# Merging the two experts' rows on TensorE before they are added to memory, two planes instead of four, and fourteen unread products

## The chip, the cores and the metric

The kernel runs on one core of one Trainium2 chip. The metric is the device time of one execution in microseconds; the time before is the median of three runs. The profile is one execution recorded by the hardware profiler; TensorE's clock has two levels in it, 1.2 GHz (granted clock 0.5) and 2.4 GHz (1.0).

## The reference, cut to what matters

The block is macaron shaped: x + 0.5 FFN(LN(x)), then x + attention(LN(x)), then x + 0.5 FFN(LN(x)), for 8 sequences of 512 tokens with 128 channels (T = 4096 tokens). The FFN is a mixture of 64 experts of inner width 88, 6 per token, plus a shared expert of width 176:

```python
scores = softmax(xf @ gate_w.T)
_, idx = top_k(scores + gate_b, 6)
# per expert, its tokens in token order; only the first CAP = 64 are kept
h  = silu(einsum('ecd,eid->eci', xb, w1)) * einsum('ecd,eid->eci', xb, w3)
yb = einsum('eci,edi->ecd', h, w2)
y  = zeros_like(xf).at[tok].add(contrib * wf[:, None])   # scatter-add by token
z  = silu(xf @ ws1.T) * (xf @ ws3.T) @ ws2.T
return (y + z).reshape(shape)
```

So each expert gives 64 rows of 128 numbers, each row is weighted with its token's score and added to its token. Two experts can hold the same token.

## The kernel before, in words

Each engine runs its own program in order; semaphores join them. `ffn(f)` stands in the program of TensorE (PE), VectorE (DVE) and ScalarE (ACT), and a loop over `f` in those of GpSimd (POOL) and SyncE (SP); f is 0 and 1 for the first and second FFN.

Routing: `norm` normalises in four groups of 1024 columns, `xT` and `logits` give the scores, DVE's `top` the six largest, and then, in four quarters h of 16 experts, `scan(h)` (DVE), `differences(h)` (PE, L722), `table(h)` (DVE, L1050), `look_up(h)` (PE, L732) and `slots(h)` (DVE, L1057) find each expert's 64 tokens. `slots` writes `tok_i`, from which POOL gathers rows, and `put_i`, where POOL adds rows. Quarters 0 and 1 run ahead of the expert turns, 2 and 3 inside turns 0 to 3.

The expert stage has 32 slots of two experts, 2s and 2s+1, on partitions 0 to 63 and 64 to 127, in NS + 2 = 34 turns (the loops at L782, L1110 and L574). In turn s PE turns the gathered rows (`xb_turn(s)`, L758), makes the hidden products of slot s-1 (`hidden`, L769) and the output products of slot s-2 (`expert_out`, L778); ACT copies the turned rows (L566) and does the silu (L572); DVE does `gate(s-1)` (L1083) and `weigh(s-2)` (L1106, two instructions of 64x128), whose semaphore `y_sb` lets POOL add the slot's 128 rows. PE waits for `y_sb` only two turns later, when it writes the bank again. The shared expert lies between: from turn 8 on, of every four turns the first two end with `shared_hidden(g, 0)` and `(g, 1)` (L705), each followed by ACT's silu (L560) and DVE's `shared_gate` (L1094), and the third with `shared_out(g)` (L718), followed by DVE's `shared_add` (L1099); the fourth has nothing. `shared_hidden(g, 1)` waits for the gate of `(g, 0)`, and `shared_out(g)` for that of `(g, 1)`. Groups 6 and 7 are made during routing (L705), multiplied in turns 3 and 4 (L1090) and brought out in turns 32 and 33.

POOL's queue is one in-order list (L458 to L470): ten gathers ahead (L466), then add(0) (L452), gather 10, add(1), and so on; the last ten adds follow each other. Each is an indirect DMA of 128 rows. Adds that may be in flight together must not meet on one row, so each token has four rows in `planes_d`: plane 2 (s mod 2) + (expert mod 2). SP zeroes the planes (`clear_planes`, 2 MB per plane): planes 0 and 1 of f = 0 at the start, 2 and 3 ahead of most of the expert weights, all four of f = 1 behind the reads of f = 0. After the last add has landed SP reads the planes in four groups of 2 MB (L345), and DVE's `update` adds each group's four planes to X (L957, four instructions of 128x1024), with statistics and normalisation behind them in the first FFN, and the store of the output (L366) behind them in the second.

## Time and profile before

| | us |
|---|---|
| median of 3 runs (lowest, highest) | 533.45 (532.67, 536.54) |
| the profiled execution | 532.9 |
| its span | 531.2 |
| PE, DVE, ACT, POOL busy in the span | 356.6, 307.6, 207.8, 237.0 |
| mean granted TensorE clock | 0.793 |

The profiled execution took 532.9 us, 1.7 us more than its span, and 0.55 us less than the median. Stages, by the time line: first FFN to 212, attention to 341, second FFN to the end; expert turns from 59 to 154 and from 396 to 489.

### The profile page before, as it was taken

The numbers are of one execution on the slowest core, as the hardware profiler recorded it, in microseconds if no ns is written. First come the engines' busy times: TensorE is split into PE (matmuls) and PEld (weight loads), VectorE is DVE, ScalarE is ACT, GpSimd is POOL, SyncE is SP. The second block draws the span as 40 slices with busy tenths as digits, with TensorE's granted clock in tenths as the row PEclk, the third lists the DMA queues.
The fourth block names the chain that finished last, engine by engine and source line by source line (L and its number), as shares of the span: only waits on it lengthen the run. The fifth ranks groups of instructions, "written<-read, shape, count | busy, mean of one in ns | idle before, by whom it ended". The sixth has DMA issues, their size and how long they took to land.

```text
span 531.2 us, 14693 instructions
## 1 busy us (share of the span) xinstructions
PE 356.6 (67%) x5808; PEld 263.3 (50%) x5812; DVE 307.6 (58%) x999; ACT 207.8 (39%) x543; POOL 237.0 (45%) x215
## 2 busy tenths in 40 slices
PE   0874589999960013598999999218848999998000
PEld 0851475666650012376788888118327667666000
DVE  6488363545430994454777775394985544545077
ACT  3983112322310067744677762169722232231000
POOL 7161747887872000403333333001537888887400
PEclk9987567999995556678999999657855699999555
DMA  8999961001015996000111111454200100100396
GB/s 272 369 268 341 318 185 15 5 11 14 5 6 218 407 401 239 2 2 2 40 40 40 40 40 49 109 218 139 61 8 8 12 11 6 17 5 6 108 426 257
DMA packets 49746, 62.64 MB, mean 118 GB/s; under 512 B 21701, under 2 KB 36248, under 8 KB 47183
## 3 DMA queue, kind: packets, MB, share of 16 engines
q1 hardware_dynamic: 37423, 60.51, 33.3%
q0 software_dynamic: 12288, 1.70, 3.2%
q8 instruction: 17, 0.28, 0.2%
q14 instruction: 18, 0.15, 0.1%
HBM read 39.53 MB, written 31.46 MB: 134 GB/s over the span
## 4 chain that ended last, share of the span: by engine, by line
PE 53%; DVE 23%; DMA 9%; ACT 6%; issue 5%; POOL 3%; SPq 1%; POOLq 0%; DVEq 0%; ACTq 0%
PE bank L769 6%; PE upper L864 5%; PE bank L705 5%; DVE X L957 5%; PE bank L718 5%; PE upper L705 4%; DMA Cb<-planes_d 4%; PE upper L778 3%; DVE Cb L1094 3%; DVE bn L962 3%; DVE Cb L1025 3%; POOL planes_d L452 3%; ACT Cb L560 2%; ACT A L508 2%; PE bank L880 2%
## 5 line engine op out<-in xcount | busy, mean ns | idle before, releaser
L452 POOL DMA_INDIRECT planes_d<-Bb,put_i x64 | 101.4, 1584 | 28.0 <-issue 14.8
L480 POOL TENSOR_TENSOR Bb<-Cb,chm 128x576 f32<-128x576 f32 x32 | 36.9, 1183 | 124.3 <-PE upper L909 69.6
L466 POOL DMA_INDIRECT A<-rows_d,tok_i x64 | 68.0, 1063 | 41.6 <-DVE put_i L1066 22.7
L672 PE MATMUL bank<-ident,A 128*128 128x128 f32 x96 | 21.3, 396 | 81.9 <-ACT A L508 65.1
L672 PEld LDWEIGHTS bank<-ident,A 128*128 128x128 f32 x96 | 17.0, 209 | 85.1 <-ACT A L508 52.3
L1106 DVE TENSOR_SCALAR Bb<-upper,A 64x128 f32<-64x128 f32 x128 | 44.4, 347 | 1.3
L1094 DVE TENSOR_TENSOR Cb<-Cb,upper 88x512 f32<-88x512 f32 x24 | 16.4, 683 | 44.8 <-ACT Cb L560 44.8
L769 PEld LDWEIGHTS bank<-ring,w1s 128*88 128x88 f32 x256 | 34.2, 191 | 8.0 <-issue 8.0
L433 POOL TENSOR_TENSOR Bb<-Eb,st 128x512 f32<-128x512 f32 x8 | 8.3, 1043 | 63.8 <-DVE st L1013 63.8
L560 ACT ACTIVATE Cb<-bank 88x512 f32<-88x512 f32 x24 | 14.2, 592 | 55.1 <-PE upper L705 55.1
L769 PE MATMUL bank<-ring,w3s 128*88 128x64 f32 x256 | 35.6, 270 | 0.0
L705 PE MATMUL bank<-XT,ws1s 128*88 128x512 f32 x56 | 32.1, 656 | 3.7 <-DVE Cb L1094 3.7
L769 PE MATMUL bank<-ring,w1s 128*88 128x64 f32 x256 | 34.1, 264 | 0.0
L1083 DVE TENSOR_TENSOR ring<-ring,bank 88x128 f32<-88x128 f32 x64 | 18.0, 281 | 26.2 <-ACT ring L572 26.1
L778 PE MATMUL upper<-w2s,ring 88*64 88x128 f32 x256 | 31.4, 328 | 0.1
L864 PE MATMUL upper<-A,Bb 32*32 32x128 f32 x1024 | 30.8, 273 | 1.0 <-issue 1.0
L769 PEld LDWEIGHTS bank<-ring,w3s 128*88 128x88 f32 x256 | 30.2, 185 | 0.0
L615 ACT ACTIVATE A<-Bb,hm 128x512 f32<-128x512 f32 x32 | 20.5, 711 | 24.1 <-PE upper L864 22.2
L705 PE MATMUL upper<-XT,ws3s 128*88 128x512 f32 x56 | 29.8, 615 | 0.0
L508 ACT ACTIVATE A<-X,st 128x128 f32<-128x128 f32 x72 | 28.6, 481 | 0.0
L957 DVE TENSOR_TENSOR X<-X,A 128x1024 f32<-128x1024 f32 x8 | 9.8, 1225 | 31.5 <-DMA A<-planes_d 31.3
L718 PE MATMUL bank<-ws2s,Cb 88*128 88x128 f32 x192 | 24.6, 281 | 3.9 <-DVE Cb L1094 3.6
(162 smaller groups left out, 804.7 us busy)
## 6 DMA issues: line engine op xcount, KB each, us to landing
planes_d<-zeros SPq DMA_DIRECT2D x8, 2048.0 KB, 15.9
rows_d<-A SPq DMA_DIRECT2D x8, 512.0 KB, 6.0
A<-planes_d SPq DMA_DIRECT2D x4, 1024.0 KB, 6.0
PL<-planes_d SPq DMA_DIRECT2D x4, 1024.0 KB, 10.0
Bb<-planes_d SPq DMA_DIRECT2D x4, 1024.0 KB, 13.7
Cb<-planes_d SPq DMA_DIRECT2D x4, 1024.0 KB, 18.0
w1s<-in_w1T SPq DMA_DIRECT2D x4, 704.0 KB
w3s<-in_w3T SPq DMA_DIRECT2D x4, 704.0 KB
```

The lines of the kernel that those rows point to most:

```text
L452: pool.indirect_dma_start(out=planes_d[f], in_=Y[:, s, :], in_offset=None, out_offset=bass.IndirectOffsetOnAxis(ap=put_i[:, s:s + 1], axis=0),
L466: pool.indirect_dma_start(out=GAT[:, t % RING, :], out_offset=None, in_=rows_d, in_offset=bass.IndirectOffsetOnAxis(ap=tok_i[:, t:t + 1], ...
L480: pool.tensor_tensor(out=VX[:, :, :, c, :].rearrange("p q h f -> p (q h) f"), in0=VN.rearrange("p q h f -> p (q h) f"), in1=chm[:, c:c + 1 ...
L508: ins = act.activation(A[:, i, :], X[:, i, :], ACT.Identity, bias=st[:, 1, i:i + 1], scale=st[:, 4, i:i + 1])
L672: ins = pe.transpose(bank[g % 2][:, (i % 4) * P:(i % 4 + 1) * P], A[:, i, :], ident[:, :])
L705: ins = pe.matmul(bank[bk][0:I, :], w[:, k * I:(k + 1) * I], XT[:, 512 * g:512 * g + 512], start=True, stop=True)
L718: ins = pe.matmul(bank[SHARED[0]][:, i * D:(i + 1) * D], hs(g)[k][:, i * P:(i + 1) * P], ws2s[:, k, :], start=(k == 0), stop=(k == 1))
L769: ins = pe.matmul(bank[2 + s % 2][0:I, cols], w[:, 2 * s + k, :], XBT[s % 2][:, CAP * k:CAP * k + CAP], start=True, stop=True)
L778: ins = pe.matmul(bank[(4, 7)[s % 2]][CAP * k:CAP * k + CAP, 0:D], GT[s % 2][:, CAP * k:CAP * k + CAP], w2s[:, 2 * s + k, :], start=True, ...
L864: ins = pe.matmul(bank[4 + g][CHUNK * c:CHUNK * c + CHUNK, q * P:(q + 1) * P] .rearrange("p (j t) -> p j t", j=4), KT[rows, t0:t0 + CHUNK] ...
L957: then(dve.tensor_tensor(xt, xt, PLANES[g].rearrange("p (i k d) -> p i k d", i=GI, k=4)[:, :, k, :], ALU.add))
L1106: ins = dve.tensor_scalar(Y[rows, s, :], bank[(4, 7)[s % 2]][rows, 0:D], GAT[rows, s % RING, col:col + 1], 0.5, ALU.mult, ALU.mult)
```

## The change

What it does:

- PE's turn becomes `xb_turn(s)`, `expert_out(s-2)`, `hidden(s-1)`, `merge(s-2)`. `merge` is one new product of 64x64 by 64x128: a matrix SAME of zeros and ones, which says which row of the second expert has the token of which row of the first, times the second expert's weighted rows. It waits for the new semaphore `weighed`, which DVE's `weigh` raises.
- DVE's turn becomes `weigh(s-2)`, `gate(s-1)`, `add_second(s-2)` (new, 64x128: the product plus the first expert's rows, which raises `y_sb`), and the rest. `weigh` no longer multiplies by 0.5.
- SAME is made per quarter: `spread(h)` (DVE, 64x512) ahead of `table(2)` and in turns 4, 10, 18; `token_rows(h)` (PE, 64x64 by 64x512) in turns 0, 5, 11, 19; `match(h)` (DVE, a compare of 64x512 from PSUM, a maximum over it, two small instructions) in turns 1, 6, 11, 19. A row of the second expert that was merged gets an index beyond the planes, and its write is dropped.
- Two planes instead of four: SP zeroes and reads half as much, the 4 MB of zeros ahead of the expert weights are gone, and `update` has two `scalar_tensor_tensor` (times 0.5, plus X) instead of four adds. The number of indirect DMAs stays.
- `keep_busy(n)` issues n products of `ident` (128x128) by 512 columns of XT into bank 2, which nobody reads: 4 ahead of `differences(0)`, 2 behind each of `differences(0)`, `look_up(0)`, `differences(1)` and `look_up(1)`, and 2 in turn 0.
- `look_up(3)` moves from turn 2 to turn 3, `table(3)` from turn 2 to turn 1 behind `slots(2)`.

```diff
+    SPREAD, ROW_TURN, MATCH = (4, 10, 18), (5, 11, 19), (6, 11, 19)
...
-        planes_d = [nc.dram_tensor(f"planes{f}_d", (4 * T, D), F32, kind="Internal").ap() for f in range(2)]
+        planes_d = [nc.dram_tensor(f"planes{f}_d", (2 * T, D), F32, kind="Internal").ap() for f in range(2)]
...
-            clear_planes(sp, 0, (0, 1))
+            clear_planes(sp, 0)
...
                 if f == 0:
-                    clear_planes(sp, 0, (2, 3))
                     for h in range(1, NQT):
...
+                            pe.wait_ge(same_ready, NQT * f + (2, 3, 3, 4, 4, 4)[g])
...
+                def keep_busy(n):
+                    for _ in range(n):
+                        pe.matmul(bank[2][:, :], ident[:, :], XT[:, 0:512], start=True, stop=True)
+
+                keep_busy(4)
                 for h in range(2):
                     differences(h)
+                    keep_busy(2)
                     look_up(h)
+                    keep_busy(2)
...
+                def token_rows(h):
+                    pe.wait_ge(rows_set, NQT * f + h + 1)
+                    if NQT * f + h:
+                        pe.wait_ge(same_ready, NQT * f + h)
+                    ss = slice(QSL * h, QSL * h + QSL)
+                    pe.matmul(bank[LOOK[1]][CAP:P, :], ones[:, :], ROWS[:, ss, :].rearrange("p s c -> p (s c)"),
+                              start=True, stop=True).then_inc(rows_ps, 1)
+
+                def merge(s):
+                    if s % QSL == 0:
+                        pe.wait_ge(same_ready, NQT * f + s // QSL + 1)
+                    pe.wait_ge(weighed, f * NS + s + 1)
+                    pe.matmul(bank[(4, 7)[s % 2]][0:CAP, D:2 * D], SAME[:, s, :], Y[CAP:P, s, :], start=True, stop=True)\
+                        .then_inc(merged, 1)
...
                 for s in range(NS + 2):
                     if s < NS:
                         xb_turn(s)
+                    if s == 2:
+                        pe.wait_ge(dr_sb, NQT * (f + 1))
+                    if s == 3:
+                        pe.wait_ge(table_ready, NQT * (f + 1))
+                    if s >= 2:
+                        expert_out(s - 2)
                     if 1 <= s <= NS:
                         hidden(s - 1)
-                    if s == 2:
-                        pe.wait_ge(dr_sb, NQT * (f + 1))
                     if s >= 2:
-                        expert_out(s - 2)
+                        merge(s - 2)
+                    if s in ROW_TURN:
+                        token_rows(1 + ROW_TURN.index(s))
                     if s == 0:
+                        keep_busy(2)
                         differences(2)
                         look_up(2)
+                        token_rows(0)
                     elif s == 1:
                         differences(3)
-                    elif s == 2:
+                    elif s == 3:
                         look_up(3)
...
-                    for k in range(4):
-                        then(dve.tensor_tensor(xt, xt, PLANES[g].rearrange("p (i k d) -> p i k d", i=GI, k=4)[:, :, k, :], ALU.add))
+                    for k in range(2):
+                        then(dve.scalar_tensor_tensor(xt, PLANES[g].rearrange("p (i k d) -> p i k d", i=GI, k=2)[:, :, k, :], 0.5,
+                                                      xt, ALU.mult, ALU.add))
...
+                def match(h):
+                    ss = slice(QSL * h, QSL * h + QSL)
+                    dve.wait_ge(rows_ps, NQT * f + h + 1)
+                    then(dve.tensor_tensor(SAME[:, ss, :], bank[LOOK[1]][CAP:P, :].rearrange("p (s c) -> p s c", s=QSL),
+                                           sl[CAP:P, 1, ss].unsqueeze(2).broadcast_to([CAP, QSL, CAP]), ALU.is_equal))
+                    then(dve.tensor_reduce(sl[CAP:P, 0, ss], SAME[:, ss, :], AX, ALU.max))
...
-                    ins.then_inc(y_sb, 1)
+                    ins.then_inc(weighed, 1)
+
+                def add_second(s):
+                    dve.wait_ge(merged, f * NS + s + 1)
+                    dve.tensor_tensor(Y[0:CAP, s, :], bank[(4, 7)[s % 2]][0:CAP, D:2 * D], Y[0:CAP, s, :], ALU.add).then_inc(y_sb, 1)
 
                 for s in range(NS + 2):
+                    if s >= 2:
+                        weigh(s - 2)
                     if 1 <= s <= NS:
                         gate(s - 1)
+                    if s == 1:
+                        match(0)
                     if s >= 2:
-                        weigh(s - 2)
+                        add_second(s - 2)
                     if s == 1:
                         slots(2)
-                    elif s == 2:
                         table(3)
                     elif s == 3:
                         slots(3)
+                    elif s in SPREAD:
+                        spread(1 + SPREAD.index(s))
+                    elif s in MATCH:
+                        match(1 + MATCH.index(s))
```

## Rows read from the trace of the kernel before

**Rows 1.** Time line (start, length, engine, operation, [idle <- its end]): adds, weighs, first gather

```profile
153.01 0.70 DVE L1106 TENSOR_SCALAR Bb<-upper,A 64x128 f32<-64x128 f32 x2
...
161.58 1.55 POOL L452 DMA_INDIRECT planes_d<-Bb,put_i  x1 [0.30 <-issue]
...
393.32 1.08 POOL L466 DMA_INDIRECT A<-rows_d,tok_i  x1 [11.36 <-DVE put_i L1066]
...
488.73 0.70 DVE L1106 TENSOR_SCALAR Bb<-upper,A 64x128 f32<-64x128 f32 x2
...
497.00 1.55 POOL L452 DMA_INDIRECT planes_d<-Bb,put_i  x1 [0.31 <-issue]
```

**Rows 2.** Busy time by stretch: PE, PEld, DVE, ACT, POOL, then PEclk, DMA share, GB/s

```profile
393.30:419.30 26.00, 21.99 (x155) 17.34 (x156) 16.11 (x47) 5.76 (x19) 21.10 (x17) 0.50 0.09 12
419.30:489.40 70.10, 65.73 (x481) 45.01 (x480) 34.87 (x96) 18.16 (x59) 56.55 (x44) 0.99 0.08 9
```

**Rows 3.** Time line behind the first FFN's adds

```profile
164.36 0.80 SPq L345 DMA_DIRECT2D A<-planes_d  x2
...
171.75 5.00 DVE L957 TENSOR_TENSOR X<-X,A 128x1024 f32<-128x1024 f32 x4 [15.76 <-DMA A<-planes_d]
...
201.81 3.19 ACT L508 ACTIVATE A<-X,st 128x128 f32<-128x128 f32 x8
...
207.17 1.92 ACT L503 ACTIVATE XT<-bank 128x512 f32<-128x512 f32 x2 [0.40 <-PE bank L672]
```

**Rows 4.** Time line behind the second FFN's adds

```profile
499.75 0.81 SPq L345 DMA_DIRECT2D A<-planes_d  x2
...
507.29 5.00 DVE L957 TENSOR_TENSOR X<-X,A 128x1024 f32<-128x1024 f32 x4 [15.58 <-DMA A<-planes_d]
...
523.01 5.00 DVE L957 TENSOR_TENSOR X<-X,Cb 128x1024 f32<-128x1024 f32 x4 [0.36 <-DMA Cb<-planes_d]
528.08 0.06 DVE L958 MEMSET st<- 128x1 f32 x1
```

**Rows 5.** Time line of four turns at full clock, first FFN

```profile
102.11 2.05 PE L718 MATMUL bank<-ws2s,Cb 88*128 88x128 f32 x16 [0.32 <-DVE Cb L1094]
...
104.00 0.27 PE L758 MATMUL upper<-ident,A 128*128 128x128 f32 x1
...
104.20 0.69 DVE L1099 SCALAR_TENSOR_TENSOR X<-bank,X 128x512 f32<-128x512 f32 x1 [1.32 <-PE bank L718]
...
105.22 0.28 DVE L1083 TENSOR_TENSOR ring<-ring,bank 88x128 f32<-88x128 f32 x1 [0.33 <-ACT ring L572]
...
106.41 1.09 PE L705 MATMUL bank<-XT,ws1s 128*88 128x512 f32 x2
...
108.39 0.59 ACT L560 ACTIVATE Cb<-bank 88x512 f32<-88x512 f32 x1 [1.98 <-PE upper L705]
...
109.02 0.68 DVE L1094 TENSOR_TENSOR Cb<-Cb,upper 88x512 f32<-88x512 f32 x1 [1.66 <-ACT Cb L560]
...
109.76 1.09 PE L705 MATMUL bank<-XT,ws1s 128*88 128x512 f32 x2 [0.32 <-DVE Cb L1094]
109.82 0.71 DVE L1106 TENSOR_SCALAR Bb<-upper,A 64x128 f32<-64x128 f32 x2
```

**Rows 6.** Time line of routing in the second FFN

```profile
384.93 0.58 ACT L543 ACTIVATE PL<-bank 88x512 f32<-88x512 f32 x1
...
387.91 0.19 PE L725 MATMUL upper<-Eb,before_b 128*128 128x16 bf16 x1 [3.51 <-DVE Eb L1046]
...
394.31 1.15 PE L739 MATMUL upper<-A,Bb 128*64 128x33 bf16 x16 [2.43 <-DVE Bb L1054]
...
395.63 0.45 PE L758 MATMUL bank<-ident,A 128*128 128x128 f32 x1 [0.16 <-DMA A<-rows_d,tok_i]
```

**Rows 7.** Time line of one turn at half clock, its start and the next one's

```profile
71.63 0.48 PE L758 MATMUL bank<-ident,A 128*128 128x128 f32 x1
...
73.79 0.48 PE L758 MATMUL upper<-ident,A 128*128 128x128 f32 x1
```

More of the change, by code:

```diff
@@ L110, in macaron_kernel @@
         plane0 = sb("plane0", [P, NS])
+        ones = sb("ones", [CAP, CAP])
         gate_s = sb("gate_s", [P, NE])
@@ L289, in macaron_kernel, with clear_planes @@
         block = ctx.enter_context(nc.Block())
-        def clear_planes(queue, f, parts=range(4)):
-            for k in parts:
+        def clear_planes(queue, f):
+            for k in range(2):
                 dst = planes_d[f][k * T:(k + 1) * T, :].rearrange("(p a i) d -> p a (i d)", p=P, i=4)
@@ L422, in _ @@
                 count(c_of_p[k * CAP:(k + 1) * CAP, :], 0, [[0, 1]], 1)
-                count(plane0[k * CAP:(k + 1) * CAP, :], k, [[0, NS // 2], [2, 2]], 0)
+                count(plane0[k * CAP:(k + 1) * CAP, :], 0, [[0, NS // 2], [1, 2]], 0)
+            then(pool.memset(ones[:, :], 1.0))
             pool.iota(slot_ce[:, :, :], pattern=[[1, CAP], [0, NE]], base=0, channel_multiplier=0,
@@ L1065, in slots, with spread @@
                     dve.tensor_copy(tok_i[:, ss], sl[:, 1, ss])
-                    dve.scalar_tensor_tensor(put_i[:, ss], sl[:, 1, ss], 4.0, plane0[:, ss], ALU.mult, ALU.add)\
+                    dve.scalar_tensor_tensor(put_i[0:CAP, ss], sl[0:CAP, 1, ss], 2.0, plane0[0:CAP, ss], ALU.mult, ALU.add)\
                         .then_inc(tokens_ready, 1)
+                def spread(h):
+                    ss = slice(QSL * h, QSL * h + QSL)
+                    dve.tensor_tensor(ROWS[:, ss, :], ident[0:CAP, 0:CAP].unsqueeze(1).broadcast_to([CAP, QSL, CAP]),
+                                      sl[0:CAP, 1, ss].unsqueeze(2).broadcast_to([CAP, QSL, CAP]), ALU.mult).then_inc(rows_set, 1)
+                def match(h):
+                    ss = slice(QSL * h, QSL * h + QSL)
+                    dve.wait_ge(rows_ps, NQT * f + h + 1)
+                    then(dve.tensor_tensor(SAME[:, ss, :], bank[LOOK[1]][CAP:P, :].rearrange("p (s c) -> p s c", s=QSL),
+                                           sl[CAP:P, 1, ss].unsqueeze(2).broadcast_to([CAP, QSL, CAP]), ALU.is_equal))
+                    then(dve.tensor_reduce(sl[CAP:P, 0, ss], SAME[:, ss, :], AX, ALU.max))
+                    then(dve.scalar_tensor_tensor(sl[CAP:P, 0, ss], sl[CAP:P, 0, ss], float(T), sl[CAP:P, 1, ss], ALU.mult, ALU.add))
+                    dve.scalar_tensor_tensor(put_i[CAP:P, ss], sl[CAP:P, 0, ss], 2.0, plane0[CAP:P, ss], ALU.mult, ALU.add)\
+                        .then_inc(same_ready, 1)
                 scan(0)
```

28 lines of the change are left out of this document (20 added, 8 removed).

## The prediction

> **What bounds the kernel now.** I read the time line of POOL first, then the busy time by stretch, then PE's, ACT's and DVE's time line through four turns, and last what follows the final add. POOL decides both expert stages. In the second FFN it issues 32 gathers and 31 adds between its first gather at 393.32 and its last add at 497.00 [rows 1]; 103.7 us over 63 DMAs is 1.65 us each, and its busy 21.10 of 26.0 us and 56.55 of 70.1 us [rows 2] leave only the gaps of issue. The last `weigh` ends at 489.43 and the last add starts at 497.00, so PE and DVE are done 7.6 us early; in the first FFN 153.71 against 161.58, 7.9 us early [rows 1]. That lead is all that PE and DVE can lose for nothing. Behind the adds stand two stretches of DMA and DVE: 164.4 to 212 and 499.8 to 531.2 [rows 3, 4].
>
> **The part that gains: two planes.** Second FFN: 2 MB land 7.54 us after the issue (499.75 to 507.29), and the fourth group's sum starts at 523.01, so a group takes (523.01 - 507.29) / 3 = 5.24 us and 2.3 us are latency [rows 4]. With half the bytes the first sum starts at 499.75 + 2.3 + 2.6 = 504.7 and the last group lands near 499.75 + 2.3 + 4 x 2.6 = 512.6, a little later beside the stores; DVE has two instructions of 1.25 us per group instead of four (5.00 us [rows 4]), if `scalar_tensor_tensor` costs what `tensor_tensor` does (per element it does within 15%: 0.69 us for 512 columns [rows 5]). So DVE ends at about 515.5 instead of 528.1: **-12.6 us**. First FFN: 2.6 us earlier start likewise. DVE's four groups take (201.81 - 171.75) / 4 = 7.5 us each, of which 2.5 go; ACT then has 0.3 + 3.19 + 1.92 = 5.4 us per group [rows 3] against DVE's 5.05 and becomes the bound by a little. Laid out group by group, ACT's last copy comes 29.5 us behind the first sum, where it came 39.6 us (it ends near 211.4): -10.1, together **-12.7 us**. Bounds of both together: -20 (instruction 1.4 us, transfers not halved in time) to -27. The clears are behind the reads or gone; nobody waits for them. The 4 MB of zeros gone ahead of the weights may let the first gathers of the first FFN land sooner, 0 to 4 us; I take this against the delay that the unread products bring there, and put the sum at 0 (-2 to +2).
>
> **The part that costs, in the repeating four turns.** In the old order PE never waits for `weigh` of the same turn. In the new one `merge` waits for it, everything of the next turn is queued behind `merge` on PE, and `weigh` is queued on DVE behind the shared expert's gate of the turn before. Count from the first product of `shared_hidden` at 106.41 [rows 5]: ACT starts at +1.98, DVE's shared gate at +2.61 and ends at +3.29; `weigh` then takes 0.71: +4.0; `merge` can start at +4.05. PE has its own turn done at 1.8 + 1.2 = +3.0 (1.2 is half of 104.00 to 106.41, two turns), so it stands idle for 1.05. The merging product has no row of its own. Below: 0.11, a quarter of the 512-column product's half (1.09 us for two [rows 5]); above: 0.5, half of that product at half clock. I take 0.22, since 128 columns are a quarter of 512 and that product takes about 0.86. The next `shared_hidden` starts at +4.27 where it started at +3.35 (109.76): +0.92, and once more for `shared_out`. Behind `shared_out` (102.11) DVE's `shared_add` starts at +2.09 and ends at +2.78 [rows 5]; `weigh` +3.5, `merge` to +3.75; then a turn without a shared part, which is `expert_out`'s result 0.5, `weigh` 0.71, `merge` 0.22 and the turning product, about 1.6; so the next `shared_hidden` starts at +5.3 instead of +4.3. Four turns: 4.27 + 4.27 + 5.3 = 13.85 us instead of 11.0. POOL needs two DMAs a turn, 2 x 1.65 = 3.3 us, 13.2 in four turns, so even where gathers and adds alternate the turns become the slower side, and in the last ten adds POOL has little to do and only waits. Turns 11 and 19 have `token_rows` and `match` besides: a product of 0.86, a compare and a maximum of 64x512 near 0.68 each as the shared gate's [rows 5], and two small ones with waits, 1.85 us of DVE ahead of the next `weigh`; PE loses about 2.2 in each. From turn 8 to the last row: 6 x 2.85 + 2 x 2.2 = **+21.5 us** (bounds +16 with the cheap product, +26 with the dear one and `add_second` above the gate's 0.28).
>
> **The first eight turns.** Before, they take 395.63 to about 419.3, 23.7 us, at granted clock 0.50 [rows 2, 6], 2.16 us each [rows 7]. Added: two unread products (1.7 us at full clock), `token_rows(0)` (0.9 to 1.7), and `merge`s that wait for a DVE which has other things first: in turn 2 `match(0)`, `slots(2)` and `table(3)` (some 3.4 us of PE idle), in turns 4 and 5 `slots(3)` and the two pairs of shared gates (0.64 each; 2.4 and 2.0), in turn 7 `match(1)` (1.7). Laying all four engines out in order with these durations gives 34.9 us if the clock is 0.5 for most of it, and 29.7 us if it is full: +11 or +6. I take **+9**, nearer the half clock. In the trace PE is busy without a break from turn 3 to turn 8, and the clock stays at 0.50 until the shared products [rows 2, 7]; the new turns have fewer products per microsecond. The Trainium skill (TensorE: Matmul & The Clock Gate, Part 1) says that the throttle is the default and that sustained activity releases it; by that rule alone these turns would run at full clock before and after, which the 0.50 of the trace does not bear out. It is rival (d).
>
> **The unread products in routing.** One is a fp32 product of 512 columns, about 0.86 us at full clock and 1.7 at half. In the second FFN the first four can start when ACT ends at 385.51 and end at 388.95, where `differences(0)` ran at 387.91: +1.0. Two more, `look_up(0)`, two, `differences(1)`, two, `look_up(1)` follow one another at 0.6 and 1.15 us: `look_up(1)` starts at 396.4 instead of 394.31, and with two more `xb_turn(0)` starts at 399.2 instead of 395.63 [rows 6]: **+3.6** (bounds +1 if half of it hides, +10 if the clock drops among them). In the first FFN PE has to wait for the first gather anyway: 0, as above.
>
> **The sum.** Second FFN: 3.6 + 9 + 21.5 = 34.1 later for the last row; the add then starts 0.85 us behind it and not 7.6, so the last add moves by +27.4. First FFN: 0 + 9 + 21.5, less 7.9 - 0.85: +23.5. Planes: -12.7 - 12.6. Together +25.6. Against the profiled execution's 532.9 that is **558.5 us**; its distance to the median, 0.55, is left out.
>
> **Rivals.**
> (a) *POOL stays the bound* (the other side: faster). If the turns lose less than the lead, 6.7 to 7.0 us per stage, the last add does not move but for the later first gather, 1.5 to 2 us. Then 532.9 - 25.3 + 3.5 = 511. It needs the `merge` waits nearly free: 32 products of 0.22 alone use 7.0 up, so it would also take a full clock in the first turns, worth up to 8 us. For it: POOL is saturated now, and PE is at half clock for eight turns. Against it: the idle 1.05 behind each shared product follows from rows. 0.14.
> (b) *Half of it*: the gate opens in the first turns, `merge` is cheap, ACT and DVE pipeline better than I lay out. +15 per stage: 532.9 + 30 - 25 = 538. 0.08, half of it within 1%.
> (c) *The clock falls in the middle.* PE is busy for 65.7 of 70.1 us at 0.99 now [rows 2]; in the new cycle it has some 11.3 of 13.85. If two cycles of six run at half clock, each loses about 7 us (two shared turns and `shared_out` at twice 1.8): +28 over both stages, 586. 0.08.
> (d) *Full clock in the first turns.* The products ahead of and in turn 0 bring the clock to 1.0 and it stays there until turn 8: +6 instead of +9 per stage, 532.9 + 25.6 - 6 = 552.5. Against it stands the 0.50 through eight dense turns. 0.15.
> (e) My forecast, with its own range of 545 to 575: 0.55.
> The range 528 to 582 leaves out most of (a) and (c). Within 1% of 533, about what a measurement of this kernel can tell from no change: 0.05; faster 0.14; slower 0.81.
>
> **What would show it.** The chain of waits should have `merge` waiting for DVE's `weigh`, about 1 us in each of the two shared turns; PE's four turns 13.8 us; POOL idle behind `add_second`, some 25 us per stage, where it has none in the second FFN now; the last add less than 1 us behind the last row; then two sums per group at 1.25 us. The forecast is wrong if the cycle stays under 13.2 us, if POOL still has a queue of adds at turn 33, or if the rows behind the adds shrink by less than 20 us.

## The result and the profile after

| | before | after |
|---|---|---|
| median of 4 runs each (lowest, highest), us | 533.06 (532.35, 536.54) | 584.4 (578.84, 588.31) |
| ratio, with its 95% interval | | 1.0864 (1.0776 to 1.0951) |
| the profiled execution, its span | 532.9, 531.2 | 580.85, 579.1 |
| PE, DVE, ACT, POOL busy | 356.6, 307.6, 207.8, 237.0 | 429.6, 326.9, 209.0, 237.4 |
| mean granted clock | 0.793 | 0.850 |

Two of the four runs of after (587.96 and 588.31 us) ran in a slower state of the chip and are left out of the ratio and of what follows, as one run of experiment 7 and one of experiment 10 are left out of their ratios; the other two took 578.84 and 580.85 us. The forecast was 558.5 us in a range of 528 to 582: the direction was right, the size (+25.6) about half of what came (+47.9 by the two profiled executions), and 580.85 lies at the very end of the range.

POOL is no longer the bound. The groups of POOL and of the new product, line by line (columns: busy, mean ns, then idle just before and what ended it):

```profile
L464 POOL DMA_INDIRECT planes_d<-Bb,put_i x64 | 101.6, 1588 | 93.6 <-DVE Bb L1176 79.8 <-issue 11.1 <-DMA planes_d<-Bb,put_i 2.8
L478 POOL DMA_INDIRECT A<-rows_d,tok_i x64 | 68.1, 1063 | 44.9 <-DVE put_i L1113 26.6 <-issue 18.3
...
L808 PE MATMUL upper<-Bb,Eb 64*64 64x128 f32 x128 | 30.9, 326 | 37.1 <-DVE Bb L1170 36.8
```

The adds cost the same (1.59 us) but POOL now stands 79.8 us waiting for `add_second` (L1176). One line below is why: TensorE is idle for 37.1 us in front of `merge` (L808), 36.8 of them waiting for `weigh` (L1170). (A product of fp32 counts as two records, so x128 are 64 merges.)

The two parts of each expert stage, from `xb_turn(0)` to turn 8 and from there to the last row, answer to [rows 2]. Busy time by stretch: PE, PEld, DVE, ACT, POOL, then PEclk, DMA share, GB/s:

```profile
63.10:100.30 37.20, 31.96 (x161) 19.33 (x162) 19.25 (x55) 5.77 (x19) 20.04 (x17) 0.55 0.16 33
100.30:197.90 97.60, 83.49 (x531) 50.15 (x532) 47.16 (x130) 19.98 (x60) 57.11 (x42) 0.96 0.07 7
425.20:460.10 34.90, 28.50 (x162) 17.59 (x161) 19.48 (x56) 5.77 (x19) 22.53 (x18) 0.65 0.07 10
460.10:555.80 95.70, 81.27 (x533) 49.70 (x533) 47.27 (x130) 18.69 (x59) 57.24 (x42) 0.99 0.06 6
```

23.7 us became 34.9, and 70.1 became 95.7. The clock is not what made the second part longer: 0.99 in it, as before. POOL's busy time in it is unchanged (57.24 against 56.55); the stretch is longer around it.

One turn with a shared part, and what stands between two of its products, which answers to [rows 5]:

```profile
477.83 1.09 PE L718 MATMUL bank<-XT,ws1s 128*88 128x512 f32 x2
...
479.82 0.59 ACT L572 ACTIVATE Cb<-bank 88x512 f32<-88x512 f32 x1 [3.28 <-PE upper L718]
...
480.44 0.68 DVE L1158 TENSOR_TENSOR Cb<-Cb,upper 88x512 f32<-88x512 f32 x1 [2.23 <-ACT Cb L572]
...
480.55 0.48 PE L792 MATMUL bank<-ring,w3s 128*88 128x64 f32 x4
...
481.05 0.71 DVE L1170 TENSOR_SCALAR Bb<-upper,A 64x128 f32<-64x128 f32 x2
...
481.81 0.43 PE L808 MATMUL upper<-Bb,Eb 64*64 64x128 f32 x2 [0.78 <-DVE Bb L1170]
482.17 0.66 PE L718 MATMUL bank<-XT,ws1s 128*88 128x512 f32 x1
```

Read it from above: the shared product, ACT's silu, DVE's shared gate; `weigh` waits in DVE's queue behind the gate, though the product that it reads (`expert_out`) is over by 480.3; PE ends its own turn at 481.03 and stands until 481.81. The next shared product starts 4.34 us behind the last, where it was 3.35 [rows 5]. The four turns take 14.37 us (477.83 to 492.20), 11.00 before.

The merge of the first slot, in the second FFN's turn 2, where `match(0)`, `slots(2)` and `table(3)` stand ahead of `weigh` on DVE:

```profile
432.05 0.69 DVE L1125 TENSOR_TENSOR Eb<-upper,sl 64x512 f32<-64x512 f32 x1
...
433.26 0.48 PE L792 MATMUL bank<-ring,w3s 128*88 128x64 f32 x4
...
435.40 0.69 DVE L1101 TENSOR_TENSOR Bb<-slot_ce,lo_b 128x1024 bf16<-128x1024 bf16 x1
436.01 0.71 DVE L1170 TENSOR_SCALAR Bb<-upper,A 64x128 f32<-64x128 f32 x2
...
436.87 0.65 PE L808 MATMUL upper<-Bb,Eb 64*64 64x128 f32 x2 [3.12 <-DVE Bb L1170]
```

Behind the adds the planes give what was expected. The second FFN's end, which answers to [rows 4]:

```profile
556.60 1.55 POOL L464 DMA_INDIRECT planes_d<-Bb,put_i  x1 [1.93 <-DVE Bb L1176]
559.35 1.76 SPq L356 DMA_DIRECT2D A<-planes_d  x4
...
564.53 2.48 DVE L1003 SCALAR_TENSOR_TENSOR X<-A,X 128x1024 f32<-128x1024 f32 x2 [6.29 <-DMA A<-planes_d]
...
573.44 2.48 DVE L1003 SCALAR_TENSOR_TENSOR X<-PL,X 128x1024 f32<-128x1024 f32 x2 [0.80 <-DMA PL<-planes_d]
575.99 0.06 DVE L1005 MEMSET st<- 128x1 f32 x1
```

From last add to the end of the span 22.5 us (34.2 before, [rows 1]), and the two instructions of 1.24 us per group that were assumed. The same stages of both executions side by side (us; a stage ends where the next begins):

| | before | after | forecast of the difference | measured |
|---|---|---|---|---|
| start of turn 0, 1st FFN | 59.16 | 63.14 | 0 | +4.0 |
| turns 0 to 8, 1st | 23.4 | 37.15 | +9 | +13.7 |
| turn 8 to last row, 1st | 71.1 | 97.6 | +21.5 | +26.5 |
| last row to last add, 1st | 7.9 | 0.85 | -7.0 | -7.0 |
| planes, behind the last add, 1st | | | -12.7 | -13.0 |
| start of turn 0, 2nd | | | +3.6 | +5.4 |
| turns 0 to 8, 2nd | 23.65 | 34.9 | +9 | +11.2 |
| turn 8 to last row, 2nd | 70.2 | 95.7 | +21.5 | +25.5 |
| last row to last add, 2nd | 7.6 | 0.8 | -6.7 | -6.7 |
| planes, behind the last add, 2nd | 34.2 | 22.5 | -12.6 | -11.7 |
| sum | | | +25.6 | +47.9 |

### The profile page after: what moved, and what is told of

Read it like the earlier page. It is cut to its first block, busy times and chain, and to the rows that moved or that the text cites. A ratio compares the mean times of both kernels' runs of the same rounds, so it can differ in the third digit from the quotient of the medians.

```text
span 579.1 us, 15197 instructions
## 1 busy us (share of the span) xinstructions
PE 429.6 (74%) x6008; PEld 289.1 (50%) x6012; DVE 326.9 (56%) x1087; ACT 209.0 (36%) x543; POOL 237.4 (41%) x216
## 3 DMA queue, kind: packets, MB, share of 16 engines
q1 hardware_dynamic: 33263, 43.73, 23.5%
## 4 chain that ended last, share of the span: by engine, by line
PE 55%; DVE 21%; ACT 9%; issue 7%; DMA 6%; SPq 1%; POOLq 0%; DVEq 0%; ACTq 0%
DVE Bb L1170 6%; PE bank L718 5%; PE upper L808 5%; PE upper L910 5%; PE bank L731 5%; PE upper L718 5%; PE bank L766 4%; ACT A L520 3%; ACT Cb L572 2%; PE bank L691 2%; PE bank L684 2%; DVE bn L1009 2%; PE bank L926 2%; PE bank L867 2%; PE bank L792 2%
## 5 line engine op out<-in xcount | busy, mean ns | idle before, releaser
L464 POOL DMA_INDIRECT planes_d<-Bb,put_i x64 | 101.6, 1588 | 93.6 <-DVE Bb L1176 79.8
L684 PE MATMUL bank<-ident,A 128*128 128x128 f32 x96 | 22.9, 418 | 62.0 <-ACT A L520 50.3
L808 PE MATMUL upper<-Bb,Eb 64*64 64x128 f32 x128 | 30.9, 326 | 37.1 <-DVE Bb L1170 36.8
L684 PEld LDWEIGHTS bank<-ident,A 128*128 128x128 f32 x96 | 18.8, 226 | 64.8 <-ACT A L520 37.4
L1170 DVE TENSOR_SCALAR Bb<-upper,A 64x128 f32<-64x128 f32 x128 | 44.4, 347 | 11.0 <-PE upper L816 9.9
L584 ACT ACTIVATE ring<-bank 88x128 f32<-88x128 f32 x64 | 17.5, 273 | 59.0 <-PE bank L792 59.0
L792 PE MATMUL bank<-ring,w1s 128*88 128x64 f32 x256 | 37.9, 278 | 0.0
L808 PEld LDWEIGHTS upper<-Bb,Eb 64*64 64x64 f32 x128 | 13.4, 146 | 46.2 <-DVE Bb L1170 34.3
L792 PEld LDWEIGHTS bank<-ring,w1s 128*88 128x88 f32 x256 | 28.7, 178 | 12.8 <-issue 8.8
L718 PE MATMUL upper<-XT,ws3s 128*88 128x512 f32 x56 | 31.0, 637 | 0.0
L766 PE MATMUL bank<-XT,ident 128*128 128x512 f32 x56 | 28.0, 632 | 2.3 <-ACT PL L555 2.3
L910 PE MATMUL upper<-A,Bb 32*32 32x128 f32 x1024 | 29.7, 271 | 0.0
## 6 DMA issues: line engine op xcount, KB each, us to landing
planes_d<-zeros SPq DMA_DIRECT2D x4, 2048.0 KB, 13.7
```

Source lines behind the costliest of these rows:

```text
L464: pool.indirect_dma_start(out=planes_d[f], in_=Y[:, s, :], in_offset=None, out_offset=bass.IndirectOffsetOnAxis(ap=put_i[:, s:s + 1], axis=0),
L684: ins = pe.transpose(bank[g % 2][:, (i % 4) * P:(i % 4 + 1) * P], A[:, i, :], ident[:, :])
L718: ins = pe.matmul(bank[bk][0:I, :], w[:, k * I:(k + 1) * I], XT[:, 512 * g:512 * g + 512], start=True, stop=True)
L766: pe.matmul(bank[2][:, :], ident[:, :], XT[:, 0:512], start=True, stop=True)
L792: ins = pe.matmul(bank[2 + s % 2][0:I, cols], w[:, 2 * s + k, :], XBT[s % 2][:, CAP * k:CAP * k + CAP], start=True, stop=True)
L808: pe.matmul(bank[(4, 7)[s % 2]][0:CAP, D:2 * D], SAME[:, s, :], Y[CAP:P, s, :], start=True, stop=True)\
```

## The experiments

Two theories stood after the result. W: the loss is the wait of `merge` for `weigh` of the same turn on PE's in-order queue. R (rival): it is the work that was added, products, DVE instructions and the fourteen unread ones, at the low clock of the first turns. All experiments change the kernel after, except where it says before.

**1 and 2. The merge a turn later, with and without the fourteen products.**

```diff
-                for s in range(NS + 2):
+                for s in range(NS + 3):
...
-                    if s >= 2:
+                    if 1 <= s <= NS:
+                        hidden(s - 1)
+                    if 2 <= s < NS + 2:
                         expert_out(s - 2)
-                    if 1 <= s <= NS:
-                        hidden(s - 1)
-                    if s >= 2:
-                        merge(s - 2)
+                    if s >= 3:
+                        merge(s - 3)
```

DVE's turn becomes gate(s-1), weigh(s-2), add_second(s-3) in the same way. The second kernel also leaves out every `keep_busy`.

> The changed kernel with each merging product one turn later: PE's turn is xb_turn(s), hidden(s-1), expert_out(s-2), merge(s-3), DVE's is gate(s-1), weigh(s-2), add_second(s-3), in 35 turns. All products stay, the unread ones too. Wait theory (the loss is that PE waits for the weigh of the same turn, behind the shared expert's gate): PE's four turns fall from 14.37 us to about 12.5 (11.0 and four products of 0.36), below POOL's 13.2, POOL issues without waits again, and the whole is 511 to 520 us. Product theory (the loss is the added work itself, wherever it stands): four turns stay near 14 and the whole near 575. Clock theory (the first turns at half clock are most of it): the first eight turns stay at 35 us and the whole is above 550.

> As e1_late without the fourteen unread products. If they only delay routing: the first gather comes 1.6 us (first FFN) and 2 to 3.6 us (second) earlier than in e1_late, POOL is the bound behind it, and the whole is 4 to 6 us below e1_late. If they help by the clock, the whole is not below e1_late.

Measured: 540.87 us (538.63 to 542.04), ratio 1.0102 (1.0059 to 1.0146), and without the products 530.16 us (529.92 to 531.89), ratio 0.9911 (0.9878 to 0.9943), the first version here with merging that is not slower than before. In both the idle time ahead of `merge` is 0.0 in the view by line. Theory W takes the larger part, but the time didn't come down to the 511 to 520 us that it asked for, and leaving the products out took 10.7 us where 4 to 6 were expected. Both intervals lie clear of 1, yet by about 1% only, less than the 2% from which a difference is called one here. The edit also puts `expert_out` behind `hidden` and `weigh` behind `gate` again, as in the kernel before; the delay and the order were not tried apart. The second kernel's trace shows what binds now. POOL's and PE's lines from its second FFN:

```profile
461.08 1.05 POOL L478 DMA_INDIRECT A<-rows_d,tok_i  x1 [0.30 <-issue]
462.44 1.59 POOL L464 DMA_INDIRECT planes_d<-Bb,put_i  x1 [0.31 <-issue]
464.33 1.05 POOL L478 DMA_INDIRECT A<-rows_d,tok_i  x1 [0.30 <-issue]
...
477.68 1.09 PE L718 MATMUL bank<-XT,ws1s 128*88 128x512 f32 x2
...
481.03 1.09 PE L718 MATMUL bank<-XT,ws1s 128*88 128x512 f32 x2
...
489.59 1.09 PE L718 MATMUL bank<-XT,ws1s 128*88 128x512 f32 x2
```

In the middle POOL is the bound again, 3.25 us a turn without a gap but that of issue. PE's four turns take 11.91 us (477.68 to 489.59), the two turns with the shared round trip 3.35 as before; so four merges that wait for nobody lengthen them by 0.91, all of it in the two turns that the round trip does not set. The merge itself is no cheaper there than where it is waited for:

```profile
487.45 0.43 PE L805 MATMUL upper<-Bb,Eb 64*64 64x128 f32 x2
487.81 0.33 PE L778 MATMUL bank<-ident,A 128*128 128x128 f32 x1
...
488.26 0.48 PE L789 MATMUL bank<-ring,w3s 128*88 128x64 f32 x4
488.86 0.44 PE L813 MATMUL upper<-w2s,ring 88*64 88x128 f32 x4
```

From its start to the next product's start it takes 0.36 us, in other turns up to 0.39. Two of them are 0.72 of the 0.91; the remaining 0.19 lie ahead of `expert_out` at 488.86, which starts 0.60 behind the product before it and not 0.41. But turns 0 to 8 take 30.3 and 31.0 us (23.5 before), all at half clock:

```profile
62.90:93.20 30.30, 28.37 (x156) 18.17 (x156) 18.43 (x54) 5.76 (x19) 15.76 (x13) 0.50 0.21 46
394.90:425.90 31.00, 28.33 (x156) 18.11 (x156) 20.13 (x60) 5.76 (x19) 20.61 (x18) 0.50 0.08 10
```

And one turn more stands at the end, so that the last row comes late and the last add starts 0.8 us behind it: POOL's lead, 7.6 us before, is gone.

**3. After without the fourteen products.**

```diff
-                keep_busy(4)
                 for h in range(2):
                     differences(h)
-                    keep_busy(2)
                     look_up(h)
-                    keep_busy(2)
...
                     if s == 0:
-                        keep_busy(2)
                         differences(2)
```

> The changed kernel without the fourteen unread products. If they buy nothing: first expert turn 1.5 to 5 us earlier per FFN and turn 0 shorter by 1.7 to 3.4 us, the whole 8 to 12 us lower, 569 to 573. If they hold the clock up for turns 0 to 2 (it is 1.0 until turn 2 in the second FFN), those turns get about 1 us longer each without them and the whole is 573 to 578. If they are worth their place, above 580.

Measured: 571.89 us (569.49 to 574.29), ratio 1.0707 (1.0662 to 1.0752). The products cost 8 us by the medians (579.8 for after's two runs against 571.9), 11.3 by the two profiled executions, of which experiment 3's is the fastest of its four, and gave nothing back. That is the first branch of the expectation. Turns 0 to 8 of this kernel (columns as above) take in sum what after's take, 71.5 against 72.1 us, at 0.50 all through:

```profile
60.30:95.70 35.40, 30.43 (x158) 18.60 (x158) 19.19 (x55) 5.78 (x19) 19.33 (x15) 0.50 0.18 42
413.30:449.40 36.10, 30.35 (x158) 18.49 (x158) 20.93 (x61) 5.78 (x19) 24.25 (x20) 0.50 0.07 10
```

From ACT's first silu behind the routing scores of the second FFN (L554, at 397.20 here and 405.37 in after) to `xb_turn(0)` it takes 16.1 us where after takes 19.8: 3.8, against the forecast's 3.6 for that term.

**4. `merge` and `add_second` behind the shared part of the same turn.**

```diff
-                    if s >= 2:
+                    part = shared_part(s)
+                    if s >= 2 and not part:
                         merge(s - 2)
...
                     elif part:
                         shared_out(part[0])
+                    if s >= 2 and part:
+                        merge(s - 2)
```

> The changed kernel with merge(s-2) and add_second(s-2) behind the shared part of the same turn, in the three turns of four that have one; the turn without a shared part and the first eight are as they were. Wait theory: the two shared turns fall from 4.34 to 3.7 us each, since weigh is done while the shared product runs, four turns from 14.37 to about 12.6, the adds then come at POOL's 3.3 us or a little faster at the end, and the whole is 545 to 556. Product theory: no change, 575 to 581.

Measured: 559.23 us (558.91 to 559.58), ratio 1.0455 (1.0421 to 1.049): 3 us above the range of the wait theory and far from the 575 of the product theory. The four turns take 12.48 us here, the turns with a shared product 3.50. By the spans this takes back 21.6 of the 39.4 us between after and the late merge of experiment 1. Of the rest, 7.2 us lie behind turn 8 (six times two cycles of 12.48 instead of 11.91), 6 in turns 0 to 8 (35.5 and 34.1 us against 33.7 and 29.7), which this edit leaves as they were, and 4 at the first FFN's start, where the two programs are alike: that part is scatter between executions.

**5. Before, with twelve of the unread products ahead of turn 0 and two in it.**

```diff
+                keep_busy(4)
                 for h in range(2):
                     differences(h)
+                    keep_busy(2)
                     look_up(h)
+                    keep_busy(2)
...
                     if s == 0:
+                        keep_busy(2)
                         differences(2)
```

> The kernel before with the fourteen unread products alone, at the same places. POOL is the bound there: the first gather comes 1.6 to 2 us later in each FFN, in the first FFN some of it is hidden in POOL's 8 us of waits, so 535 to 538 us. If the products brought the clock up through the first turns, POOL's waits in the first FFN would go and the whole be 530 or below.

Measured: 539.7 us (536.5 to 541.48), ratio 1.0119 (1.0055 to 1.0182). That is above the 535 to 538 expected. Here the products cost 5 to 6 us, less than in the changed kernel: in the first FFN POOL's first gather and turn 0 come 1.6 and 2.9 us later, in the second `xb_turn(0)` 3.8 us later, counted as in experiment 3. Turns 0 to 8 are 24.9 and 23.1 us; before, they were 23.4 and 23.65, so the products bring no clock to those turns that would shorten them.

**6. After, with one more unread product of 512 columns in each of turns 1 to 7.**

```diff
+                    if 1 <= s < 8:
+                        pe.matmul(bank[(0, 5)[(s + 1) % 2]][:, :], ident[:, :], XT[:, 0:512], start=True, stop=True)
                     if s >= 2:
                         merge(s - 2)
```

> The changed kernel with one more unread product of 512 columns in each of turns 1 to 7, ahead of the merging product, where PE waits for DVE (into a bank that is free there). Clock theory: the granted clock stays 1.0 through turns 1 to 7, the eight turns take 30 us instead of 35 and 37, and the whole is 568 to 573. Queue theory (DVE's queue of match, slots, table and early gates bounds these turns): the clock is 1.0 but the eight turns stay within 2 us of 35, and the whole is 577 to 583. If the products come on top, above 583.

Measured: 569.67 us (564.3 to 572.09), ratio 1.0661 (1.058 to 1.0741). Turns 0 to 8:

```profile
61.40:92.80 31.40, 26.51 (x174) 14.49 (x175) 19.00 (x55) 5.77 (x19) 18.84 (x16) 1.00 0.18 36
413.80:445.20 31.40, 26.50 (x176) 14.45 (x175) 19.34 (x56) 5.77 (x19) 21.39 (x18) 1.00 0.08 10
```

With seven products more (6.0 us at full clock) both stretches are 3.5 to 5.8 us shorter than after's, at 1.00, 9.2 us together; time and clock are what the clock theory asked for. In the kernel after, unread products in the turns themselves win 10 us by the medians (11 by the spans), where those ahead of the turns lose 8 to 11. A reading of it, which experiment 8 bears out: they win where they lie in front of a wait of PE for `weigh`.

**7. The planes alone, on the kernel before.** Planes 2 and 3 are written and cleared but neither read nor summed, so the rows of odd slots are left out of the result.

```diff
-        PLANES = (A_flat, PL[:, :], Bb[:, 0:T], Cb[:, 0:T])
+        HP = T // 2
+        PLANES = (A_flat[:, 0:HP], A_flat[:, HP:T], PL[:, 0:HP], PL[:, HP:T])
...
-                    src = planes_d[f].rearrange("(p i k) d -> p i (k d)", p=P, k=4)
+                    src = planes_d[f].rearrange("(p i k) d -> p i (k d)", p=P, k=4)[:, :, 0:2 * D]
...
-                    for k in range(4):
+                    for k in range(2):
```

> The kernel before, with its four planes written and cleared as they were, but only planes 0 and 1 read back and summed (so the rows of odd slots are left out of the result). It gives the price of the planes alone, without any merging. From the two traces the stretch between last add and attention became 13.0 us shorter and the stretch behind the second FFN's last add 11.7 us. Theory (these are the planes' and the stages themselves need not change): 533.4 - 24.7 = about 509 us, turns 0 to 8 still 23.5 us, last adds as before. Rival (part of the 24.7 came from something else, such as POOL being drained at the end, or DMA beside the stores): 515 to 522.

Measured: 512.82 us (511.58 to 519.62), ratio 0.9596 (0.9553 to 0.9639); span 511.6. The end of its time line:

```profile
488.10 1.55 POOL L453 DMA_INDIRECT planes_d<-Bb,put_i  x1 [0.30 <-issue]
490.85 2.01 SPq L346 DMA_DIRECT2D A<-planes_d  x4
...
495.89 2.48 DVE L958 TENSOR_TENSOR X<-X,A 128x1024 f32<-128x1024 f32 x2 [12.07 <-DMA A<-planes_d]
...
505.91 2.49 DVE L958 TENSOR_TENSOR X<-X,PL 128x1024 f32<-128x1024 f32 x2 [0.25 <-DMA PL<-planes_d]
```

-13.1 us behind the first FFN's last add and -10.7 behind the second's; turns 0 to 8 23.6 in both, the last adds 1.86 apart as in [rows 1]. So the planes' gain in these two stretches is there without any merging. The time, 512.8, fell between the 509 of the theory and the 515 of the rival: the span is 4 us above the sum of the two gains, with 1.9 at the start of turn 0 in the first FFN and 2.5 ahead of turn 0 in the second, where the clock rose later. The memory traffic is not quite that of two planes, since all four are cleared and the reads skip over two.

**8. The late merge without the fourteen, and one unread product in each of turns 1 to 7** (the edit of experiment 6 on the kernel of experiment 2).

> The merge a turn later, none of the fourteen products, but one unread product of 512 columns in each of turns 1 to 7. In the kernel it starts from, turns 0 to 8 take 30.3 and 31.0 us at half clock, 2.78 us for a turn with nothing else in it; POOL starts the last add 0.8 us behind its row. Theory (the half clock is what makes merges and row products dear there, and nothing hides it): at full clock a turn is 1.2 + 0.23 + 0.86 = 2.3 us, the two row products are cheaper by 1.5: turns 0 to 8 become 26 to 27 us, and the time 530.2 - 8 = 522, at most 526 if the clock takes two or three turns to rise. Rival 1 (POOL's two DMAs per turn bind from there on, 13.0 us in four turns against PE's 11.9): the turns shorten but the last add does not move, 530. Rival 2 (clock does not rise, since the turns wait for DVE's tables): 530 + 2 x 6 = 542.

Measured: 528.86 us (524.74 to 531.31), ratio 0.9887 (0.9824 to 0.995). Turns 0 to 8 took 31.4 and 31.8 us, against 30.3 and 31.0. The first FFN's, in two halves:

```profile
60.90:75.00 14.10, 12.62 (x51) 6.57 (x53) 5.92 (x17) 2.47 (x7) 4.07 (x4) 0.50 0.35 93
75.00:92.30 17.30, 16.81 (x119) 9.85 (x117) 12.14 (x36) 3.31 (x12) 10.38 (x8) 0.98 0.08 7
```

The clock did rise, but only after 14 us, and without an idle stretch to lie in each product costs its 0.86 us (1.7 in the first half). Neither the theory's 522 to 526 nor a rival came out: what the clock gives in these turns the products take.

**9. The two output products of shared groups 6 and 7 a turn later** (on the kernel of experiment 2), behind the last merge.

```diff
-            if NS <= s < NS + EARLY:
-                return NSH - EARLY + s - NS, 2
+            if NS < s <= NS + EARLY:
+                return NSH - EARLY + s - NS - 1, 2
```

> The merge a turn later, none of the fourteen products, and the two output products of shared groups 6 and 7 (2.05 us each) one turn later, in turns 33 and 34, the last one behind the last merge instead of before it. In the kernel it starts from the last row is ready at 507.37 and the last add starts 0.78 later, landing 2.8 us after that. Theory (PE's queue sets the last row): the last row comes 2 us sooner, the shared product ends beside the landing of the add; 2 us per FFN, 530.2 - 4 = 526. Rival (POOL or the wait of an add for the one before the last sets the end): no change, 530. Rival 2 (the shared sum becomes what the reads wait for): 530 to 532.

Measured: 528.9 us (525.44 to 530.65), ratio 0.9892 (0.9844 to 0.994), against 0.9911 in experiment 2: no difference that can be told from none, and not the 526 of the theory. The trace shows the second rival at work:

```profile
505.24 3.75 PE L731 MATMUL bank<-ws2s,PL 88*128 88x128 f32 x16 [0.26 <-DVE X L1159]
506.06 1.55 POOL L464 DMA_INDIRECT planes_d<-Bb,put_i  x1 [0.62 <-issue]
509.03 0.69 DVE L1159 SCALAR_TENSOR_TENSOR X<-bank,X 128x512 f32<-128x512 f32 x1 [3.73 <-PE bank L731]
509.81 1.76 SPq L356 DMA_DIRECT2D A<-planes_d  x4
```

The last add starts 1.1 us earlier, counted from turn 0, but the product behind the last merge takes 3.75 us instead of 2.05, at a granted clock of 0.50 (1.00 until 501, 0.76 from there to 505.2), and the reads now wait for its sum at 509.72 and not for the add's landing.

**10 and 11. Two planes and no merging: each add waits for the one before.** Before, with plane = expert mod 2, so that two adds in flight would meet; POOL gathers ten, then six slots ahead.

```diff
-                    n = f * (NS // 2) + s // 2
+                    n = f * (NS // 2) + (s + 1) // 2
                     if n:
-                        pool.wait_ge(added[s % 2], 16 * n)
+                        pool.wait_ge(added[(s + 1) % 2], 16 * n)
```

> The kernel before with two planes and no merging at all: plane = expert mod 2, and each add waits for the landing of the one before it (2.8 us from issue by the list of DMA issues) instead of the one before that, so no two adds in flight can meet. Theory: while gathers and adds alternate, POOL needs 3.25 us a turn and the landing is covered; the last ten adds stand alone and take about 3.0 instead of 1.86 us each, +10 us per FFN, against -12 from the planes: 533.1 - 24.7 + 20 = 529 us. Rival (the wait costs every add, 64 times some 0.5 us): 545 to 560.

> As the one before it, but POOL gathers six slots ahead instead of ten, so only the last six adds stand alone. Theory: +1.1 x 5 = 5.7 us per FFN instead of 10, and the turns are not held up by the gathers: 533.1 - 24.7 + 11.4 = 520 us. Rival 1 (six ahead is too few: PE waits for gathers in the first turns, where add(0) is issued earlier in POOL's queue): 525 to 535. Rival 2 (landing is never covered): as above, 545 or more.

Measured: 567.66 us (562.94 to 574.22), ratio 1.0505 (1.0373 to 1.0636), and 570.97 us (568.96 to 573.88), ratio 1.0621 (1.0517 to 1.0724). Both theories were far off (529 and 520 us); what came is the rivals' mechanism, a wait in every turn, and more of it than their 545 to 560. Adds of the first of the two where gathers lie between, then where none does:

```profile
449.44 1.05 POOL L466 DMA_INDIRECT A<-rows_d,tok_i  x1 [0.30 <-issue]
451.42 1.59 POOL L452 DMA_INDIRECT planes_d<-Bb,put_i  x1 [0.93 <-DMA planes_d<-Bb,put_i]
...
518.76 1.55 POOL L452 DMA_INDIRECT planes_d<-Bb,put_i  x1 [2.43 <-DMA planes_d<-Bb,put_i]
522.42 1.55 POOL L452 DMA_INDIRECT planes_d<-Bb,put_i  x1 [2.11 <-DMA planes_d<-Bb,put_i]
```

An add behind an add needs 3.5 to 4.0 us from start to start, where the expectation had about 3.0 from the 2.8 of the list of DMA issues, and the gather of 1.35 us between two does not cover it: a turn with both takes 3.6 to 4.2 us around these rows where experiment 2's takes 3.25. What two planes need, with or without a merge, is a way to keep two adds in flight; the merging on TensorE is such a way.

**12. A better order of the first turns** (on experiment 9): `token_rows(0)` in turn 2 instead of 0, `match(0)` in turn 2 instead of 1, behind `table(3)`.

```diff
                         look_up(2)
-                        token_rows(0)
...
+                    elif s == 2:
+                        token_rows(0)
```

> The merge a turn later, none of the fourteen products, the shared output products of groups 6 and 7 in turns 33 and 34, and besides token_rows(0) moved from turn 0 to turn 2 and match(0) from turn 1 to turn 2 (behind table(3)). Theory (in the first turns PE and DVE wait for each other: PE starts turn 1 only behind the 1.97 us of token_rows, and in turn 3 waits 1.16 us for table(3), which stands behind match(0) on DVE): turns 0 to 8 take 28 to 29 us instead of 30.3 and 31.1, and the time is 528.9 - 4 = 525. Rival (every product there costs its own time at half clock, wherever it stands, and merge(0) waits for match(0) instead): turns 0 to 8 as before, 529.

Measured: 530.76 us (525.91 to 533.05, 12 runs), ratio 0.9909 (0.9874 to 0.9944). Turns 0 to 8 are 29.3 and 30.0 us, each 1 us shorter, 1 us short of what the theory asked; in the time it does not show. The lowest of the merging kernels thus all lie together at about -1% (experiments 2, 8, 9 and 12), and the plainest of them is a late merge and no unread products.

Four of the kernels, put in a row by the spans of their profiled executions, split the result:

| step | span | difference |
|---|---|---|
| before | 531.2 | |
| planes alone (7) | 511.6 | -19.6 |
| and merging a turn late, nobody waiting for it (2) | 530.2 | +18.6 |
| and merging in the turn itself, with its wait (3) | 567.8 | +37.6 |
| and the fourteen unread products (after) | 579.1 | +11.3 |

By the medians the last three steps are +18, +42 and +8 us. Single executions of one kernel lie up to 5 us apart, so no step is known better than to some us. The wait step has its witness in the trace: 35.6 us of idle ahead of `merge` in the kernel of experiment 3, none in that of experiment 2:

```profile
L805 PE MATMUL upper<-Bb,Eb 64*64 64x128 f32 x128 | 30.8, 325 | 36.0 <-DVE Bb L1166 35.6
```

```profile
L805 PE MATMUL upper<-Bb,Eb 64*64 64x128 f32 x128 | 30.5, 323 | 0.0
```

## Why the prediction was right in direction and short in size

- **The bound.** That the lead of 7.6 and 7.9 us is all PE and DVE can lose, and that POOL then waits for `add_second`, is shown: -7.0 and -6.7 as forecast, and POOL's 79.8 us of wait (the forecast's sign was some 25 us per stage). Rivals (a) and (b) fell with it: (a)'s time of 511 is what experiment 7 measured (512.8), but for the planes alone; it needed `merge` waits near zero, and they are 36.8 us.
- **The planes.** -12.7 and -12.6 forecast, -13.0 and -11.7 measured, and -13.1 and -10.7 in experiment 7. The latency of 2.3 us and a half of 5.24 us per group held within a microsecond in this sum.
- **The repeating four turns.** The mechanism was right (`merge` waits behind the shared gate and `weigh`, 0.78 to 0.88 us of idle where 1.05 was worked out, `weigh` ending at +3.93 where +4.0 was). The mis-sized term is the merge itself: "I take 0.22" for a product that holds the next product off for 0.36 us (481.81 to 482.17). Four times 0.14 is 0.56, and 13.85 + 0.56 = 14.4 is the 14.37 measured. It is no matter of the place: in experiment 2, where nobody waits for it, it takes 0.36 to 0.39 as well. The Trainium skill (TensorE: Matmul & The Clock Gate, Part 2, phase 5) says that products issued back to back overlap the drain of one with the fill of the next, and that a single isolated one can't hide its drain; these rows show no difference between the two places. The 0.22 was a quarter of a product of 512 columns, as if time went by columns alone, and the lower bound of 0.11 rests on taking the two records of "1.09 us for two" for two products, where they are one. A nearer row stands in the trace of before, `expert_out`, two products (four records) with 64 columns loaded and 128 streamed as in the merge; the next product starts 0.37 us behind it, at 106.41 [rows 5]:

```profile
106.04 0.44 PE L778 MATMUL upper<-w2s,ring 88*64 88x128 f32 x4
```

  What makes 0.36 of it was not tried. Six cycles with 0.52 more than forecast make 3.1 us per stage; the stages came to +25.5 and +26.5 for +21.5, 9 us over both. The rest lies in the last turns and in cycles that ran partly at half clock: 0.92 in the second FFN's first, 0.88 and 0.90 in the first FFN's first two.
- **The first eight turns.** "I take +9", between +11 (half clock) and +6 (full). Measured +13.7 and +11.2 at 0.55 and 0.65. The layout at half clock, 34.9 us, is the second FFN's to a tenth, though part of that stretch ran at full clock, so the agreement is in part luck, and 2.2 short of the first's. The step that failed was to go below it, towards rival (d), for which no row spoke. (d) itself did not come: with the fourteen products the clock fell back within the first turns (0.55 and 0.65 over the eight), and in experiment 5 it did not shorten them (24.9 and 23.1 us). It was 1.00 throughout only in experiment 6, with one more product in each turn. Experiment 2 splits the term: of the 12 us in experiment 3, 7 remain when no product waits for a `weigh` of its own turn (30.7 against 23.5 us), with PE busy for 28.4 of 30.3 us at half clock, and 5 go with that wait.
- **The start of turn 0.** In the second FFN +3.8 from ACT's first silu behind the routing scores, against +3.6; the other 1.6 of the +5.4 lie ahead of it. In the first FFN the forecast was 0 and the value +4.0. The products are not free there: POOL's first gather stands behind `slots(0)`, which they delay, and its idle time grows from 11.38 us to 13.01, 1.6 us, in experiment 5 too. The zeros gone ahead of the weights, reckoned at "0 to 4 us sooner", did not show: from the first gather to turn 0 it takes 7.1 us before, 7.6 in after and 8.3 in experiments 2 and 3, which have no products. Before, then experiment 3:

```profile
59.16 0.47 PE L758 MATMUL bank<-ident,A 128*128 128x128 f32 x1 [4.93 <-DMA A<-rows_d,tok_i]
```

```profile
60.30 0.48 PE L778 MATMUL bank<-ident,A 128*128 128x128 f32 x1 [6.19 <-DMA A<-rows_d,tok_i]
```

  How the rest of the +4.0 divides is not known, for this stretch scatters by as much: experiments 2 and 3 have the same program up to there and start turn 0 at 62.87 and 60.30, after and experiment 4 at 63.14 and 66.47.
- **Rival (c)**, the clock falling in the middle, had nearly the right time (586, against 580.85) for the wrong reason: the clock was 0.96 and 0.99 there, against 0.97 and 0.99 before. A sum that comes out right is no evidence for its mechanism.

The added errors: 4.0 + 1.8 at the two starts, 4.7 + 2.2 in the first turns, 5.0 + 4.0 in the cycles, 0.6 in the planes, which is the 22.3 us between forecast and result. Nearly all of it is on one side, so the errors did not cancel. They have no single cause that is shown: the merge at 0.22 is one, the +9 chosen between +6 and +11 another, and the starts are in part scatter. At the dear ends of the two large terms (+11, +26) the sum would have been 571.5.

## What to carry to other kernels

When a step is added that waits for another engine in the same turn, price it by the whole way round, that wait plus the time in which the small product holds the next one off, and take that time from a row of a product as small, not from a share of a wide one. Then look whether the turn after can take it, which here was worth 38 to 42 us for one turn more at the end. A saving behind a saturated engine (the planes, -4%) is easily spent again in front of it, so measure it alone first. Unread products won only where the engine stood idle in front of a wait (experiment 6); ahead of the turns they cost 5 to 11 us, and in turns without such waits they changed nothing (experiment 8).

## What the runs showed of the hardware

- A 64x64 by 64x128 fp32 product holds TensorE's next product off for 0.36 to 0.39 us at full clock, whether it had to wait (after) or not (experiment 2); at half clock it lengthens a turn by 0.62 us (2.78 us a turn in the second experiment against 2.16 [rows 7]).
- TensorE was busy for 28.4 of 30.3 us in turns 0 to 8 of experiment 2 and stayed at 0.50, while with one 512-column product more per turn it had 1.00 at a busy time of 26.5 of 31.4 us. The stretch with the larger busy time had the lower clock. The Trainium skill (TensorE: Matmul & The Clock Gate, Part 1) has sustained activity release the throttle; experiment 6 agrees with it, and the row of experiment 2 does not, if activity is what the profile counts as busy.
- An accumulating indirect DMA can be issued every 1.86 us with two in flight, but one that waits for the one before comes only every 3.5 to 4.0 us. The Trainium skill (DMA: Bandwidth & Descriptors, Anatomy of one DMA) says that a DMA's fixed cost of about 2 us is mostly the wait for completion, long above all when the target is HBM; start to start less the 1.55 us of issue, 2.0 to 2.4 us here with the planes in DRAM, is of that size; how it divides was not measured.
- The same shared product takes 2.05 us in the turns and 3.75 as the last work of the stage (experiment 9): the granted clock was 1.00 up to 501 and 0.50 from 505.2 on, though TensorE was busy for 3.90 of the 4.20 us between.
